# A fused layernorm, depool and gated feed-forward kernel: its hi/lo subtractions of weights and first inputs, and its last addition, change from VectorE to GpSimd

## The reference

```
n  = layernorm(x)
h  = rmsnorm(n, g_res) @ W_in.T + b_in
s  = associative scan over rows of rmsnorm(ctx, g_init)[:, :512], with a fixed decay
x2 = x + h + s[plug]             # plug: row index from the cumulated patch lengths
y  = layernorm(x2), y_prev = y shifted by one row
r  = sigmoid((mu_r*y + (1-mu_r)*y_prev) @ W_r.T)
k  = relu((mu_k*y + (1-mu_k)*y_prev) @ W_k.T) ** 2
out = x2 + r * (k @ W_v.T)
```

## Time and profile before

| what | value |
|---|---|
| time, median of 3 runs | 801.11 us (798.61 to 802.12) |
| profiled execution: its time | 801.11 us |
| profiled execution: span in the trace | 799.5 us |
| PE busy | 760.9 us (95%) |
| DVE busy | 588.3 us (74%) |
| ACT busy | 398.3 us (50%) |
| POOL busy | 201.8 us (25%) |
| transfers | 85.80 MB, mean 107 GB/s |
| granted TensorE clock, mean | 0.984 of full speed |

### The profile page before, as it was taken

The page is one execution under the profiler, slowest core; times in us unless marked ns, Lnnn a source line. Parts: engine busy times, 40 slices in busy tenths (PEclk is TensorE's granted clock), DMA queues, the critical chain, the costliest instruction groups (busy, mean ns, idle before and its releaser), DMA issues.

```text
span 799.5 us, 10975 instructions
## 1 busy us (share of the span) xinstructions
PE 760.9 (95%) x3458; PEld 620.9 (78%) x3459; DVE 588.3 (74%) x1074; ACT 398.3 (50%) x649; POOL 201.8 (25%) x169
## 2 busy tenths in 40 slices
PE   4679999899999999999999999999999999999997
PEld 1467688787888878788888888888887888878876
DVE  6878978778596777869596786968778685878462
ACT  3226744454564535556454545645453564544750
POOL 6134231402323140232313032231403223140000
PEclk9598999999999999999999999999999999999999
DMA  8385071350806226080623507071341707131011
GB/s 304 123 237 121 26 194 56 86 166 15 236 1 170 81 67 182 14 236 0 162 88 86 164 34 216 0 190 60 102 148 40 210 0 199 52 87 33 1 53 53
DMA packets 44733, 85.80 MB, mean 107 GB/s; under 512 B 5104, under 2 KB 5104, under 8 KB 44688
## 3 DMA queue, kind: packets, MB, share of 16 engines
q1 hardware_dynamic: 30864, 63.02, 22.2%
q0 software_dynamic: 9216, 16.78, 12.8%
q10 hardware_dynamic: 4608, 5.51, 1.9%
HBM read 63.51 MB, written 21.79 MB: 107 GB/s over the span
## 4 chain that ended last, share of the span: by engine, by line
PE 57%; DVE 17%; DMA 8%; issue 8%; POOL 4%; ACT 3%; DVEq 0%; POOLq 0%; ACTq 0%
PE bank L442 19%; PE bank L443 18%; PE bank L444 18%; DMA ring<-s_rows,patch_now 7%; POOL ring L402 3%; DVE bn_a L850 2%; DVE bn_b L960 2%; PE bank L546 2%; DVE normed L973 2%; DVE xk_lo L821 2%; DVE ring L954 2%; DVE scratch L924 1%; DMA s_rows<-scanned 1%; DVE xr_lo L821 1%; DVE bn_c L868 1%
## 5 line engine op out<-in xcount | busy, mean ns | idle before, releaser
L402 POOL DMA_INDIRECT ring<-s_rows,patch_now x64 | 105.9, 1655 | 159.5 <-DMA s_rows<-scanned 128.8
L924 DVE SCALAR_TENSOR_TENSOR scratch<-turned,mus,scratch 128x512 f32<-128x512 f32 x128 | 94.6, 750 | 35.6 <-ACT scratch L682 22.0
L442 PE MATMUL bank<-wi_hi,xt_hi 128*128 128x512 f32 x256 | 103.4, 404 | 0.7 <-DVE wi_lo L821 0.7
L442 PE MATMUL bank<-xk_hi,wk_hi 128*128 128x512 f32 x256 | 100.1, 391 | 3.0 <-DVE xk_lo L821 3.0
L443 PE MATMUL bank<-wi_lo,xt_hi 128*128 128x512 f32 x256 | 101.8, 398 | 0.0
L444 PE MATMUL bank<-wi_hi,xt_lo 128*128 128x512 f32 x256 | 101.4, 396 | 0.0
L442 PE MATMUL bank<-wv_hi,xr_hi 128*128 128x512 f32 x240 | 95.9, 399 | 5.7 <-DVE xr_lo L821 5.5
L442 PE MATMUL bank<-wr_hi,xr_hi 128*128 128x512 f32 x256 | 99.7, 390 | 0.0
L443 PE MATMUL bank<-xk_lo,wk_hi 128*128 128x512 f32 x256 | 99.6, 389 | 0.0
L444 PE MATMUL bank<-xk_hi,wk_lo 128*128 128x512 f32 x256 | 99.6, 389 | 0.0
L444 PE MATMUL bank<-wr_hi,xr_lo 128*128 128x512 f32 x256 | 99.6, 389 | 0.0
(11 more groups left out here) (116 smaller groups left out, 1309.0 us busy)
## 6 DMA issues: line engine op xcount, KB each, us to landing
xt<-in_x_turned SPq DMA_DIRECT2D x16, 1024.0 KB, 10.5
ring<-in_x SPq DMA_DIRECT2D x16, 1024.0 KB, 13.1
out<-gate SPq DMA_DIRECT2D x64, 256.0 KB
ctx_rows<-in_ctx SPq DMA_DIRECT2D x16, 512.0 KB
s_rows<-scanned ACTq DMA_DIRECT2D x19, 256.0 KB, 2.1
gate<-in_L_xattn_W_in SPq DMA_DIRECT2D x1, 1024.0 KB, 7.5
turned<-in_L_ffn_W_r SPq DMA_DIRECT2D x1, 1024.0 KB, 16.9
ring<-s_rows,patch_now POOLq DMA_INDIRECT x64
```

The source lines that it names most:

```text
L402: pool.indirect_dma_start(ring[b.slot][:, t, :], None, s_rows[:, :], bass.IndirectOffsetOnAxis(ap=patch_now[:, t:t + 1], axis=0), compute_ ...
L442: nc.tensor.matmul(where, lhs_hi, rhs_hi, start=start, stop=False)
L924: nc.vector.scalar_tensor_tensor(scratch[:, 2 + i % 2, :], turned[:, c, 1:S + 1], mus[:, which, c:c + 1], scratch[:, i % 2, :], ALU.mult, ...
```

## The change

GpSimd takes over from DVE: `weight_lo` for all four weights, `x_lo` for the first batch and for half of batch 1, and every `add_out`. The subtractions and additions are the same instructions on the same operands, now issued by the other engine. On GpSimd the first two add_out of b stand ahead of far(new) and add_patches(new), the last two behind them. The allocation order in SBUF changes too.

```diff
@@ GpSimd: new helpers
+            def weight_lo(w, first=0, last=C):
+                for c in range(first, last):
+                    pool.wait_ge(w_hi_ready[w], c + 1)
+                    nc.gpsimd.tensor_tensor(wt_lo[w][:, c, :], staged[w][:, c, :], f32(wt_hi[w][:, c, :]),
+                                            ALU.subtract).then_inc(w_lo_ready[w], 1)
+            def x_lo(b, n):
+                reached(pool, xt_lo_ready, b, 2, n)
+                reached(pool, xt_hi_ready, b, 2, n + 1)
+                nc.gpsimd.tensor_tensor(xt_lo[:, 2 * n:2 * n + 2, :], xt[:, 2 * n:2 * n + 2, :],
+                                        f32(xt_hi[:, 2 * n:2 * n + 2, :]), ALU.subtract).then_inc(xt_lo_ready, 1)
+            def add_out(b, t):
+                reached(pool, gated, b, T, t + 1)
+                nc.gpsimd.tensor_tensor(gate[:, t, :], gate[:, t, :], ring[b.slot][:, t, :], ALU.add).then_inc(out_ready, 1)
@@ GpSimd: iteration
+                if b.exists(B):
+                    add_out(b, 0)
+                    add_out(b, 1)
                 if new.exists(B):
                     far(new)
                     add_patches(new)
                 if is_first(nxt):
                     root_a(new)
+                    weight_lo(WK)
+                    weight_lo(WV)
+                if b.exists(B):
+                    add_out(b, 2)
+                    add_out(b, 3)
@@ GpSimd: setup
             nc.gpsimd.memset(ones_b, 1.0).then_inc(ones_ready, 1)
+            x_lo(Batch(0, 0), 0)
             pool.wait_ge(half_ready, 1)
             root_c(Batch(0, 0))
+            x_lo(Batch(0, 0), 1)
+            weight_lo(WIN)
             pool.wait_ge(table_ready, 2)
...
             root_a(Batch(0, 0))
+            weight_lo(WR, 0, C // 2)
             root_c(Batch(0, 1))
+            x_lo(Batch(0, 1), 1)
+            weight_lo(WR, C // 2, C)
             batches(pool, iteration, B)
@@ DVE: iteration 0
-                if is_first(b):
-                    weight_lo(WK)
-                    weight_lo(WV)
@@ DVE: every iteration
-                    add_out(b, 0)
-                    add_out(b, 1)
                     gating(b, 2)
                     gating(b, 3)
-                    add_out(b, 2)
-                    add_out(b, 3)
@@ DVE: setup
                 if c == 0:
                     u_low(Batch(0, 0))
-                if c == 0:
-                    x_lo(Batch(0, 0), 0)
-                else:
-                    weight_lo(WIN, c - 1, c)
-                if c == 1:
-                    x_lo(Batch(0, 0), 1)
...
-            weight_lo(WIN, C - 1, C)
...
             x_lo(Batch(0, 1), 0)
-            weight_lo(WR)
-            x_lo(Batch(0, 1), 1)
```

More of the change, by code:

```diff
@@ L113, in build @@
         s_rows = nc.dram_tensor("s_rows", [S, D], F32, kind="Internal").ap()
-        ident = sb("ident", [P, P])
-        bn_a, mv_a, rs_a = (sb(f"{n}_a", [P, T, k]) for n, k in (("bn", 6), ("mv", 2), ("rs", 1)))
-        v_a = sb("v_a", [P, RING, T])
-        bn_b, mv_b, v_b, rs_b = (sb(f"{n}_b", [P, T, k]) for n, k in (("bn", 6), ("mv", 2), ("v", 1), ("rs", 1)))
-        bn_c, mv_c, v_c, rs_c = (sb(f"{n}_c", [P, k]) for n, k in (("bn", 12), ("mv", 2), ("v", 2), ("rs", 1)))
-        mus = sb("mus", [P, 4, C])
-        g_cols = sb("g_cols", [P, C])
-        count_i = sb("count_i", [P, W32], I32)
-        half = sb("half", [P, T])
-        far_table = sb("far_table", [1, 2 * B], I32)
-        far_f = sb("far_f", [1, 3, B])
-        patch_of = sb("patch_of", [P, B, T], U32)
         wt_hi = [sb(f"w{n}_hi", [P, C, D], F32R) for n in "irkv"]
@@ L137, in build @@
         normed = sb("normed", [P, T, D])
+        turned = sb("turned", [P, C, S + 1])
         xk_hi, xk_lo = sb("xk_hi", [P, C, S], F32R), sb("xk_lo", [P, C, S], F32R)
@@ L150, in build @@
         g_ctx = sb("g_ctx", [P, D])
+        ident = sb("ident", [P, P])
+        average = sb("average", [P, P])
+        decay = sb("decay", [P, 2, P])
         decay_hi, decay_lo = sb("decay_hi", [P, 2, P], F32R), sb("decay_lo", [P, 2, P], F32R)
-        decay = sb("decay", [P, 2, P])
-        average = sb("average", [P, P])
-        turned = sb("turned", [P, C, S + 1])
+        mus = sb("mus", [P, 4, C])
+        g_cols = sb("g_cols", [P, C])
+        count_i = sb("count_i", [P, W32], I32)
+        half = sb("half", [P, T])
+        bn_a, mv_a, rs_a = (sb(f"{n}_a", [P, T, k]) for n, k in (("bn", 6), ("mv", 2), ("rs", 1)))
+        v_a = sb("v_a", [P, RING, T])
+        bn_b, mv_b, v_b, rs_b = (sb(f"{n}_b", [P, T, k]) for n, k in (("bn", 6), ("mv", 2), ("v", 1), ("rs", 1)))
+        bn_c, mv_c, v_c, rs_c = (sb(f"{n}_c", [P, k]) for n, k in (("bn", 12), ("mv", 2), ("v", 2), ("rs", 1)))
+        far_table = sb("far_table", [1, 2 * B], I32)
+        far_f = sb("far_f", [1, 3, B])
         index_i = sb("index_i", [P, 3, T * B], I32)
-        patch_now = sb("patch_now", [P, T], U32)
+        patch_of, patch_now = sb("patch_of", [P, B, T], U32), sb("patch_now", [P, T], U32)
         lens = [normed[0:B, 0:2, :].rearrange("p a b -> p (a b)").bitcast(I32),
@@ L837, in x_lo @@
                     f32(xt_hi[:, 2 * n:2 * n + 2, :])).then_inc(xt_lo_ready, 1)
-            def weight_lo(w, first=0, last=C):
-                for c in range(first, last):
-                    dve.wait_ge(w_hi_ready[w], c + 1)
-                    low(wt_lo[w][:, c, :], staged[w][:, c, :], f32(wt_hi[w][:, c, :])).then_inc(w_lo_ready[w], 1)
-            def add_out(b, t):
-                reached(dve, gated, b, T, t + 1)
-                nc.vector.tensor_tensor(gate[:, t, :], gate[:, t, :], ring[b.slot][:, t, :], ALU.add).then_inc(out_ready, 1)
             def statistics_a(b, t):
```

## The result

| | before | changed |
|---|---|---|
| time, median | 799.86 us (796.85 to 802.12, 4 runs) | 813.17 us (812.39 to 813.49, 4 runs) |
| profiled execution: span | 799.5 us | 810.8 us |

The ratio is 1.017, with a 95% interval of 1.014 to 1.020. The prediction was 788.6 us, with a range of 780 to 800.5. Even the sign is wrong. The executions of the kernel before differ among themselves by up to 6 us.

A forecast was written before the change was run, and what follows sets the result against it. The prediction took PE as the bound, busy 760.9 of 799.5 us. From 801.1 us it took 8.5 (middle), 3 (setup) and 1 (end), giving 788.6 us, with a range of 780 to 800.5.

The forecast's parts named there:

- Part 5: End: PE's 1.21 us wait for xk_lo(3) in the last batch goes, -1 us (0 to -1.2); new SBUF order 0.
- Part 1: Loop: two GpSimd additions ahead of the patches, 1.3 us each, first patch issue at about -1.4, cost +0.2 us.
- Part 2: Loop: two additions behind the patches; loads leave at about +10 instead of +3.4, patches move alone, x just hidden.
- (b): Rival, loop: patches no faster, slowed by their own gathers and not by the loads; 797 us, chance 0.08.
- (c): Rival, loop: additions wait for DVE's mixing, x loads come late and become the bound; about 820 us, chance 0.13.
- (a): Rival, loop and setup: GpSimd additions of 1.75 us hold DVE twice, L1133 near 32; about 798 us, chance 0.13.
- Part 3: Loop: GpSimd's additions hold DVE's mixing, ending it at +14.8, using up 1.5 us slack; middle -8.5 us (0 to -10.5).
- Part 4: Setup: DVE sheds subtractions and PE waits less, against DVE being held by GpSimd; -3 us (-6.5 to +1).

The follow-up runs named there:

- the early part by itself: Kernel before, old allocation order, with only the low parts of W_in and of the first batch's turned x moved to GpSimd: 799.23 us, ratio 1.001.
- the kernel with the pad of 224 bytes: Changed kernel, new allocation order, plus 224 unused bytes behind `turned`, putting xk and xr at distance 0 modulo 256 from the weights: 798.76 us, ratio 1.001.

## Why the prediction was wrong

**The step that failed** is the last sentence of Part 5: "The new SBUF order: nothing that a row can price, 0". It is worth +14 us in this kernel. No row of before shows an operand at another distance, so no row could have priced it, but it was also given no bound and no rival: a part of the change that touches every matmul was set to 0 for lack of a row. The size of the risk was to be had from rows: PE is busy for 95% of the span, and 1% of that is 7.6 us.

Without the layout the changed kernel takes 799.0 us, which lies in the range of the prediction. That would have been luck: -9.6 us in the middle, nearly as forecast, and +9.3 at the two ends, where -4 was forecast.

**Part 1 (additions ahead of the patches): the size right, the reason not.** 1.3 us each, as taken; first issue at -1.1 against -1.6, 0.5 us where 0.2 was put. But the additions end at -3.5, and GpSimd then waits 2.23 us for the stored scan. Its terms, -3.3 and 0.91 us, give -2.4 and not the -1.4 that it has. What is later is the stored scan: it lands 2.66 us behind its issue in this iteration, where it took 1.98 before.

**Part 2 (loads leave later, patches alone): right.** Loads at +9.8 (predicted +10), DVE's waits for the patches 7.3 us in place of 50.6, statistics of x without a wait. The kernel with only the held loads shows that this, and not a lighter DVE, is what pays. The patches without loads need 11.0 to 12.2 us there, where 11.4 was taken. Rivals (b) and (c) fall, and so does (a) for the middle.

**Part 3 (the port in the loop): right, with the open side now shown.** No row of before had DVE held. In the changed kernel it is held while the two additions run, from 399.26 to 402.41, and mixing ends at +14.2 (predicted +14.8). The slack carries it. It was more than the 1.5 us that were read: 427.81 is the start of DVE's gating, and PE's scan starts at 428.29, which makes 2.0. The middle without the layout came to -9.6, predicted -8.5.

**Part 4 (setup): wrong, +6.4 for -3.** The bound on the bad side was +1. The term of W_k and W_v is the one: their 5 us were counted as shed by DVE, and their price only as a delay of batch 0's sigmoid. The rows show that DVE had those 5 us idle, and that DVE loses not one of GpSimd's instructions but the rest of the run of eight, 7.2 us. The early half was about right in size: DVE is held twice, for 2.78 and 2.75 us in the rows below, the cumulated sum starts at 31.41, the "near 32" of rival (a), and PE starts again 1.8 us later for it, though the early part by itself leaves 0.5 us at the second turning. But the first instruction that is held isn't the one named. It is the shift of the index table (L1105, 0.63 us before), which reads one SBUF tensor, and so does L1136, for which PE waits: 1.31 us beside GpSimd's run for W_in, 0.41 before. Counting SBUF inputs wasn't enough to find what GpSimd holds.

```profile
14.97 2.78 DVE L1105 TENSOR_SCALAR index_i<-index_i 128x64 int32<-128x64 int32 x1
...
24.02 2.75 DVE L902 SCALAR_TENSOR_TENSOR u<-ctx_rows,rs_c,g_ctx 128x512 f32<-128x512 f32 x1 [0.16 <-POOL rs_c L376]
...
33.32 1.31 DVE L1136 TENSOR_SCALAR normed<-normed 16x512 f32<-16x512 f32 x1
...
34.68 0.42 PE L661 MATMUL bank<-ident,normed 16*128 16x16 f32 x4 [1.95 <-DVE normed L1136]
```

**Part 5 (the end): wrong, +2.5 for -1** in the changed kernel. The additions left DVE's queue and held DVE all the same. The layout has 1.6 us of it (35.07 us for the shortened period where 34.41 stood, and 144 slow matmuls behind it), the final addition 0.7 and the longer wait 0.2.

The sum by spans: +6.4 to the second turning, +2.4 in the middle (-9.6, and the longer matmuls, 0.99 us in each of the last 12 periods), +2.5 at the end: 11.3, which is 810.8 - 799.5.

## What to carry to other kernels

When a diff reorders allocations, compare the addresses of each matmul's two operands: at distances that are no multiple of 256 bytes a 128x512 float32r matmul took 229 to 234 ns in place of 227, and where TensorE is the bound that is paid nearly in full (14.2 us of the 15 by this count). Work moved to GpSimd is not off DVE's path if DVE has an instruction with two SBUF operands beside it, and here two with one operand were held as well: price it as a stop of DVE for the whole run of GpSimd's instructions, and ask first whether the operation on DVE was standing in a wait anyway. And if a gain comes from a transfer that starts later, a wait in the queue that issues it buys it without moving any work.

## What the hardware showed that I had not expected

- The distance of the two operands of a matmul: 226.7 to 227.1 ns at multiples of 256 bytes, 229 to 234 at the others that were tried, with no other engine at work. Whether other shapes or types behave alike wasn't tried.
- GpSimd's run of instructions with two SBUF inputs keeps DVE's out until it ends: 6.9 and 7.2 us for one instruction of 0.75, and 8.7 with short memsets in between. The Trainium skill ("SBUF — State Buffer", "Who interferes with whom") has the loser wait for one instruction of the other; these rows have it wait for a run of instructions that follow each other without a gap.
- After a stop of PE of 1.8 us at the end of two kernels the granted clock went down to its 1.2 GHz level for 3.4 us. After 1.2 and 1.5 us, in the kernel before and the changed one, it didn't, nor after 1.76 us at the same place in the kernel with the pad of 224 bytes. A short wait can cost twice, and whether it does can't be told from its length here.
